# Graph layer with linear attention, 1 core: query denominators four chunks at a time in eight partitions, and the remainders of two weight slabs on VectorE

## The reference, cut to what matters

```python
phiQ = elu_plus_one(Q)                      # Q = xn @ Wq.T + bq, heads of 64
phiK = elu_plus_one(K)
S = jnp.einsum('bhki,bhkj->bhij', phiK, V)
Z = phiK.sum(axis=-2)
num = jnp.einsum('bhqi,bhij->bhqj', phiQ, S)
denom = jnp.einsum('bhqi,bhi->bhq', phiQ, Z)[..., None] + EPS
context = (num / denom).transpose(0, 2, 1, 3).reshape(B, L, E)
```

## Time and profile before

| | |
|---|---|
| median of three timed runs | 995.62 us |
| the profiled execution | 995.84 us |
| its span | 994.1 us |
| TensorE matmul busy | 975.2 us, 98% |
| VectorE | 543.9 us, 55% |
| ScalarE | 293.6 us, 30% |
| GpSimd | 142.4 us, 14% |
| bytes moved by DMA | 86.78 MB |
| query chunks | about 296 to 425 us |

### The profile page before, as it was taken

How to read it: one execution, slowest core, us unless ns; L and a number is a source line. 1 busy time by engine, 2 the same in 40 slices (tenths; PEclk the granted TensorE clock), 3 DMA queues, 4 the chain that set the end, 5 groups by cost and what they waited for, 6 DMA issues and landing times.

```text
span 994.1 us, 13325 instructions
## 1 busy us (share of the span) xinstructions
PE 975.2 (98%) x4860; PEld 824.4 (83%) x4860; DVE 543.9 (55%) x1067; ACT 293.6 (30%) x585; POOL 142.4 (14%) x191
## 2 busy tenths in 40 slices
PE   5999999999999999999999999999999999999998
PEld 4887888888889989978786788767788999999986
DVE  6886578777763888782113556447557212122354
ACT  6873122232133343341213221114113312135300
POOL 7101001001011050050300000000201103064100
PEclk9999999999999999999999999999999999999999
DMA  7412013113021022122201465535422302010053
GB/s 269 150 49 86 5 30 117 28 31 100 16 77 36 26 90 73 52 69 95 96 12 55 147 204 172 157 119 186 170 80 90 123 1 85 1 43 1 22 190 139
DMA packets 46979, 86.78 MB, mean 87 GB/s; under 512 B 19036, under 2 KB 23388, under 8 KB 46896
## 3 DMA queue, kind: packets, MB, share of 16 engines
q1 hardware_dynamic: 38416, 57.28, 17.5%
q0 software_dynamic: 8480, 28.45, 8.7%
HBM read 61.62 MB, written 24.09 MB: 86 GB/s over the span
## 4 chain that ended last, share of the span: by engine, by line
PE 92%; DVE 3%; DMA 2%; ACT 1%; issue 1%; POOL 1%; SPq 0%; DVEq 0%; ACTq 0%; POOLq 0%
PE PS L1431 11%; PE PS L1433 11%; PE PS L1432 11%; PE PS L1552 9%; PE PS L1553 9%; PE PS L1554 9%; PE PS L1610 5%; PE PS L1612 4%; PE PS L1630 3%; PE PS L1631 3%; PE PS L1629 3%; PE PS L1471 2%; PE PS L1446 2%; PE PS L1683 2%; PE PS L1682 2%; PE PS L1681 2%
## 5 line engine op out<-in xcount | busy, mean ns | idle before, releaser
L1431 PE MATMUL PS<-ring,act_t 128*128 128x512 f32 (+1 forms) x480 | 194.7, 406 | 1.3 <-POOL ring L443 0.6
L1433 PE MATMUL PS<-ring,act_t 128*128 128x512 f32 (+1 forms) x480 | 190.7, 397 | 0.0
L1432 PE MATMUL PS<-ring,act_t 128*128 128x512 f32 (+1 forms) x480 | 190.3, 396 | 0.0
L1552 PE MATMUL PS<-act_t,ring 128*128 128x416 f32 (+1 forms) x432 | 159.3, 369 | 1.4 <-POOL ring L443 1.3
L1553 PE MATMUL PS<-act_t,ring 128*128 128x416 f32 (+1 forms) x432 | 152.2, 352 | 0.0
L1554 PE MATMUL PS<-act_t,ring 128*128 128x416 f32 (+1 forms) x432 | 151.7, 351 | 0.0
L1431 PEld LDWEIGHTS PS<-ring,act_t 128*128 128x128 f32 (+1 forms) x480 | 89.8, 187 | 23.9 <-POOL ring L443 1.6
L1433 PEld LDWEIGHTS PS<-ring,act_t 128*128 128x128 f32 (+1 forms) x480 | 89.5, 186 | 22.4
L1432 PEld LDWEIGHTS PS<-ring,act_t 128*128 128x128 f32 (+1 forms) x480 | 89.9, 187 | 21.2 <-issue 0.5
L1552 PEld LDWEIGHTS PS<-act_t,ring 128*128 128x128 f32 x432 | 81.3, 188 | 6.8 <-issue 3.4
L1553 PEld LDWEIGHTS PS<-act_t,ring 128*128 128x128 f32 x432 | 81.4, 188 | 4.0 <-issue 3.4
(11 more groups left out here) (195 smaller groups left out, 1650.7 us busy)
## 6 DMA issues: line engine op xcount, KB each, us to landing
stage_x<-in_wslices_dram POOLq DMA_DIRECT2D x54, 256.0 KB, 4.2
stage<-in_wslices_dram POOLq DMA_DIRECT2D x42, 256.0 KB, 3.7
xr<-x_d SPq DMA_DIRECT2D x18, 512.0 KB, 3.6
phin_d<-phiq SPq DMA_DIRECT2D x8, 625.0 KB, 3.1
xrow<-in_x_dram SPq DMA_DIRECT2D x9, 512.0 KB, 3.6
xh<-in_x_dram SPq DMA_DIRECT2D x18, 256.0 KB
x_d<-xh SPq DMA_DIRECT2D x18, 256.0 KB
x_d<-xr SPq DMA_DIRECT2D x9, 512.0 KB, 3.0
```

Of the source, the lines that this page charges most:

```text
L1431: pe.matmul(out_ap, node_rows(0, k, t), ring[:, slot(k0 + k), 0, :], start=(k == 0), stop=False)
L1432: pe.matmul(out_ap, node_rows(1, k, t), ring[:, slot(k0 + k), 0, :], start=False, stop=False)
L1433: ins = pe.matmul(out_ap, node_rows(0, k, t), ring[:, slot(k0 + k), 1, :], start=False, stop=(k == KD - 1))
L1552: pe.matmul(out_ap, w[0], x_t[:, 0, k, o:o + n], start=(k == 0), stop=False)
```

## The change

- The key sums take one column per feature tile and are split into high half and remainder (`z_hl`, eight columns for each chunk's place in its group; the unused ones are zero). `phi_split` (ScalarE) and `phi_rest` (VectorE) split phiq into `phi_hl` (two buffers).
- A chunk's denominator is three fp32r passes with eight stationary columns. Four chunks of the same rows of x (four feature tiles) form a group and add into eight partitions of one bank. The order of the chunks changes to `q_chunk`; chunks 11 and 23 are still the last of their slab.
- Copy and reciprocal run once for a group, on eight partitions. The reciprocals go to DRAM (`rec_d`) and come back spread over 64 partitions a head, in four parts with a semaphore each. The multiply of chunk i is 8 chunks behind; phiq has nine buffers of a chunk, each stored by itself.
- Remainders of slices 42 to 57 are made by VectorE, eight after q_add(10) and eight after q_add(22). GpSimd keeps the loads. ScalarE makes all eight high halves ahead of its step of chunk 11 (23).

```diff
-PHI_BUFS = 3
+PHI_BUFS = 9
+PHI_LAG = 8
+def q_chunk(i):
+    s, r = divmod(i, 12)
+    return 4 * s + r % 4, r // 4
...
@@ sync
+            def rec_store(g):
+                n = CHUNKS[g % 3][1]
+                sp.wait_ge(rec_ready, g + 1)
+                sp.dma_start(rec_d[g].rearrange("a b n -> (a b) n")[:, 0:n], rec[0:8, 0:n]).then_inc(rec_stored, 16)
+            def rec_spread(g, j):
+                n = CHUNKS[g % 3][1]
+                sp.wait_ge(rec_stored, 16 * (g + 1))
+                if g >= 1:
+                    sp.wait_ge(phin_ready, 4 * (g - 1) + j + 1)
+                for h in range(2):
+                    sp.dma_start(rec_all[64 * h:64 * h + 64, j, 0:n],
+                                 rec_d[g, j, h:h + 1, 0:n].to_broadcast([64, n])).then_inc(rec_in[j], 16)
+            for i in range(24 + PHI_LAG):
+                g, late = divmod(i - 6, 4)
+                if late == 0 and 0 <= g < 6:
+                    rec_store(g)
+                if i >= PHI_LAG:
+                    phin_store(i - PHI_LAG)
+                if late == 0 and 0 <= g < 6:
+                    for j in range(3):
+                        rec_spread(g, j)
+                if late == 1 and 0 <= g < 6:
+                    rec_spread(g, 3)
...
@@ gpsimd
-            slab_rest(42)
-            slab_rest(50)
+            for n in range(42, 58):
+                reload(n)
...
@@ scalar
+            def phi_split(i):
+                n = CHUNKS[q_chunk(i)[1]][1]
+                act.wait_ge(phiq_ready, i + 1)
                 if i >= 2:
+                    act.wait_ge(phi_used, i - 1)
+                nc.scalar.activation(phi_hl[:, 0, i % 2, 0:n], phiq[:, i % PHI_BUFS, 0:n], ACT.Copy).then_inc(phi_hi, 1)
...
                 if i % 12 == 11:
-                    for k in range(42 + 8 * (i // 12), 48 + 8 * (i // 12)):
+                    for k in range(42 + 8 * (i // 12), 50 + 8 * (i // 12)):
                         hi(k)
...
-                if i >= 2:
-                    den_copy(i - 2)
+                if i >= 1:
+                    phi_split(i - 1)
+                if i >= 5 and i % 4 == 1:
+                    den_copy((i - 5) // 4)
...
+            phi_split(23)
             act.wait_ge(deg_copied, 1)
...
@@ vector
+            def phi_rest(i):
+                n = CHUNKS[q_chunk(i)[1]][1]
+                dve.wait_ge(phi_hi, i + 1)
+                dve.tensor_tensor(phi_hl[:, 1, i % 2, 0:n], phiq[:, i % PHI_BUFS, 0:n],
+                                  phi_hl[:, 0, i % 2, 0:n].bitcast(F32), ALU.subtract).then_inc(phi_lo, 1)
...
             for i in range(24):
                 q_min(i)
-                if i >= 3:
-                    den_invert(i - 3)
+                if i == 1:
+                    z_rest()
+                if i >= 1:
+                    phi_rest(i - 1)
+                if i >= 6 and i % 4 == 2:
+                    den_invert((i - 6) // 4)
+                if i >= PHI_LAG:
+                    den_apply(i - PHI_LAG)
                 q_add(i)
-                if i >= 3:
-                    den_apply(i - 3)
+                if i % 12 == 10:
+                    for n in range(42 + 8 * (i // 12), 50 + 8 * (i // 12)):
+                        weight_lo(dve, n)
...
             for t in range(NT):
                 h_lo(0, t)
-                if t < 3:
-                    den_invert(21 + t)
-                    den_apply(21 + t)
+                if t == 2:
+                    den_invert(5)
+                if t < PHI_LAG:
+                    den_apply(24 - PHI_LAG + t)
...
@@ tensor
-                for i in range(2):
-                    u = UNIT["z", i]
-                    b = open_unit(u)
-                    for j in range(4):
-                        ins = pe.matmul(PS[:, b, P * j:P * (j + 1)], ksum[:, P * (4 * i + j):P * (4 * i + j + 1)], ones[:],
-                                        start=True, stop=True)
-                    ins.then_inc(acc_full, 1)
+                u = UNIT["z", 0]
+                b = open_unit(u)
+                for f in range(KD):
+                    ins = pe.matmul(PS[:, b, f:f + 1], ksum[:, P * f:P * (f + 1)], ones[:, 0:1], start=True, stop=True)
+                ins.then_inc(acc_full, 1)
...
             def denominator(i):
...
+                pe.wait_ge(phi_lo, i + 1)
+                if j == 0 and g >= 2:
+                    pe.wait_ge(den_read, g - 1)
+                for z, b in ((0, 0), (0, 1), (1, 0)):
+                    ins = pe.matmul(PS[0:8, 3 + g % 2, 0:n], z_hl[:, z, i // 12, 8 * j:8 * j + 8], phi_hl[:, b, i % 2, 0:n],
+                                    start=(j == 0 and z + b == 0), stop=(j == 3 and z == 1))
+                ins.then_inc(phi_used, 1)
```

More of the change, by code:

```diff
@@ L108, in rows @@
     return min(P, N - t * P)
+def q_chunk(i):
+    s, r = divmod(i, 12)
+    return 4 * s + r % 4, r // 4
 def units():
     u = [("kv", s, t) for s in range(4) for t in range(NT)]
-    u += [("q", 0, 0), ("z", 0), ("z", 1)]
-    u += [("q", f, c) for f in range(KD) for c in range(3) if f or c]
+    u += [("q", 0, 0), ("z", 0)]
+    u += [("q", *q_chunk(i)) for i in range(1, 24)]
     u += [("h", 0, t) for t in range(NT)]
@@ L219, in build @@
         with ExitStack() as r2:
+            sb("pad3", [P, 2 * NT * 512 - 4 * 418], F32, r2)
+            phi_hl = sb("phi_hl", [P, 2, 2, 418], F32R, r2)
+        with ExitStack() as r2:
             hs = sb("hs", [P, 2, NT, 512], F32R, r2)
@@ L321, in build @@
         phiq_ready = sem("phiq_ready")
-        den_done = sem("den_done")
+        z_hi = sem("z_hi")
+        phi_hi = sem("phi_hi")
+        phi_lo = sem("phi_lo")
+        phi_used = sem("phi_used")
+        rec_stored = sem("rec_stored")
+        rec_in = [sem(f"rec_in{j}") for j in range(4)]
         den_read = sem("den_read")
@@ L498, in _ @@
                         keys_load(dt + KEY_BUFS)
-                if step >= 40 and (step - 40) % 3 == 2 and (step - 40) // 3 >= 1:
-                    phin_store((step - 40) // 3 - 1)
-            phin_store(KD - 1)
+            for i in range(24 + PHI_LAG):
[9 more added lines that the diff above has]
+                    rec_spread(g, 3)
             for b in range(PHI_BUFS):
-                sp.wait_ge(phin_stored[b], 16 * len(range(b, KD, PHI_BUFS)))
+                sp.wait_ge(phin_stored[b], 16 * len(range(b, 24, PHI_BUFS)))
             for b in range(2):
@@ L684, in _ @@
             for b in range(PHI_BUFS):
-                pool.wait_ge(phin_stored[b], 16 * len(range(b, KD, PHI_BUFS)))
+                pool.wait_ge(phin_stored[b], 16 * len(range(b, 24, PHI_BUFS)))
             for b in range(2):
@@ L1207, in q_add, with z_rest @@
                                   ALU.add).then_inc(phiq_ready, 1)
[L1209 to L1212, removed]
-            def den_apply(i):
[L1215 to L1219, removed]
+            def z_rest():
+                u = UNIT["z", 0]
+                dve.wait_ge(z_hi, 1)
+                for g in range(2):
+                    o = slice(64 * g, 64 * g + 64)
+                    z_out = dve.tensor_tensor(z_hl[o, 1, :, g:g + 31:10], PS[o, bank(u), 0:KD].rearrange("p (a b) -> p a b", a=2),
+                                              z_hl[o, 0, :, g:g + 31:10].bitcast(F32), ALU.subtract)
+                z_out.then_inc(acc_free[bank(u)], 1)
@@ L1220, in den_apply @@
+            def den_apply(i):
+                n = CHUNKS[q_chunk(i)[1]][1]
+                dve.wait_ge(rec_in[i % 4], 32 * (i // 4 + 1))
+                dve.tensor_tensor(phiq[:, i % PHI_BUFS, 0:n], phiq[:, i % PHI_BUFS, 0:n], rec_all[:, i % 4, 0:n],
                                   ALU.mult).then_inc(phin_ready, 1)
@@ L1234, in _ @@
                     dve.tensor_copy(deg[0:last, 0, NT - 1:NT], PS[0:last, 7, NT - 1:NT]).then_inc(deg_copied, 1)
+            phi_rest(23)
             dve.wait_ge(root_deg, 1)
```

85 lines of the change are left out of this document (42 added, 43 removed).

## The result

The changed kernel takes 1012.81 us (median of six runs, 1011.86 to 1013.65) where the kernel before took 996.51 (six runs, 995.32 to 998.20). The ratio is 1.0163, with a 95% interval of 1.0152 to 1.0173: slower, by 16 us where I had forecast 2.5. The profiled execution of the changed kernel has a span of 1010.9 us, that of the kernel before 994.1: +16.9 us.

A forecast was written before the change was run, and what follows sets the result against it. TensorE, busy for 98% of the span, was taken as the bound. Slab changes +6.2, passes −3.4 and key sums −0.3 gave +2.5 us: 998.3 us for the profiled execution, 998.1 as median, range 995.5 to 1003.

The forecast's parts named there:

- part 3: Remainders of both slab changes on VectorE: +9.77 us of TensorE waits, −3.54 us of GpSimd waits gone, net +6.23 us.
- Rival (b): At the slab changes phi_rest(10) comes in time, only 2.3 us of weight waits remain: 990.8 us, faster; chance 0.07.
- (d): Rival: the waits are real but 1 to 3 us smaller altogether, 996.5 us, no difference to be told; chance 0.12.
- part 1: Denominators on TensorE as three fp32r passes: 0.14 us saved each, 3.4 us in all; key sums 0.3 us.
- Rival (c): The eight-column passes of the denominators save nothing: 1001.5 us; chance 0.06.
- the key sums: TensorE's sixteen passes with one moving column instead of 128: 0.3 us saved, bounds 0 and 1.1 us.
- part 2: Inverse per group and its spread through DRAM: hidden; at the end, the last store before GpSimd's loads, nothing or 0.3 us.
- rival (a): TensorE's clock drops to half behind the 3.6 us waits, 4 us each: one 1002, both 1006; chance 0.12.

The follow-up runs named there:

- x1_early_switch: Changed kernel plus one GpSimd tensor_tensor on one column right behind the partition_all_reduce; 1002.67 us, ratio 1.0060 to the kernel before.
- x3_dve_rest_only: Kernel before with the remainders of slices 42 to 57 moved to VectorE, fp32 denominators kept; 992.04 us, ratio 0.9954.
- x4_filler: x1_early_switch plus twelve unused 416-column passes ahead of the wait in denominator(10) and in denominator(22); 998.48 us, ratio 1.0023 to the kernel before.
- x6_order: x1_early_switch with VectorE reordered: inverse ahead of phi_rest, remainders split four, two and two; 989.65 us, ratio 0.9934 to the kernel before.
- x2_gpsimd_rest: Changed kernel with the remainders of slices 42 to 57 back on GpSimd; 1001.68 us, ratio 1.0061 to the kernel before.
- x8_gpsimd_rest_inv_first: x2_gpsimd_rest with VectorE's inverse ahead of phi_rest; 997.31 us, ratio 1.0010 to the kernel before.
- x5_lag3: x1_early_switch with each denominator one chunk later and the group copies one step later; 992.03 us, ratio 0.9958 to the kernel before.

## Why the prediction was wrong

**Right: the waits at the slab changes (part 3).** The chain was forecast as first remainder 6.27 us after q_min(10), 0.80 us apart, q_min(11) at 12.46, phi_rest(10) from 14.74. VectorE's timeline of the changed kernel:

```profile
353.42 0.65 DVE L1233 TENSOR_SCALAR qmin<-PS,bq_sb 128x416 f32<-128x416 f32 x1 [1.30 <-PE PS L1611]
355.63 0.59 DVE L1258 TENSOR_TENSOR phi_hl<-phiq,phi_hl 128x416 fp32r<-128x416 f32 x1 [1.55 <-ACT phi_hl L858]
356.14 2.73 DVE L1264 RECIPROCAL rec<-rec 8x416 f32<-8x416 f32 x1
...
359.75 1.47 DVE L460 TENSOR_TENSOR ring<-stage,ring 128x512 fp32r<-128x512 f32 x2
361.32 4.67 DVE L460 TENSOR_TENSOR ring<-stage_x,ring 128x512 fp32r<-128x512 f32 x6
365.90 0.65 DVE L1233 TENSOR_SCALAR qmin<-PS,bq_sb 128x416 f32<-128x416 f32 x1
368.10 0.59 DVE L1258 TENSOR_TENSOR phi_hl<-phiq,phi_hl 128x416 fp32r<-128x416 f32 x1 [1.55 <-ACT phi_hl L858]
```

Measured from 353.42: 6.33, 12.48 and 14.68. Chunk 12 lost 10.50 − 5.12 = 5.38 us (forecast 5.40), h(0,0) 10.86 − 6.14 = 4.7 (4.4). Net of the old stalls the two are +6.6 us (5.38 + 4.72 − 3.54), forecast +6.2. Rival (b) didn't come about, nor did (d). That the inverse keeps its length with eight partitions (2.73 us) was right too.

**Right: the passes (part 1).** 5.12 to 5.13 us a chunk, 0.14 less than before in each. Rival (c) is out: three passes with eight stationary columns still step at 0.19 us. The Trainium skill, page "TensorE: Matmul & The Clock Gate", section "LDWEIGHTS (loading the stationary operand)", has a weight load go by its columns. The records of the loads are shorter with eight columns than with 128 (88 ns for 188, median), though by far less than in proportion, and the step of the passes doesn't change with them. The formula that I had taken from the section "Back-to-back issue gap" of that page of the Trainium skill is given there for a single pass by itself, not for a stream of passes. The saving that I worked out from it, 4.3 us, is 4.4 if added up rightly, and the measured one is 3.3. **A small miss:** the key sums saved nothing, 303.08 − 301.37 = 1.71 us for 1.70; I had taken 0.3.

**Wrong: the end of part 2, "Nothing, or 0.3 us".** This is the step that cost most: the term was put at nothing, and h(1,0) took 9.9 us longer. I checked that the last store would land before GpSimd's remainders were due, and took GpSimd to be ready from then on. But taking slices 42 to 57 from it in part 3 also took away its first elementwise instruction behind the all-reduce, and with it the early moment at which the gap behind the configuration records passed unseen. That gap, 9.4 us, is about 9 of the 9.9 us: x1_early_switch brings h(1,0) from 15.58 back to 6.63. The remaining 1.0 us is the store itself, which I had sized too small: GpSimd's loads were issued 4.8 us behind the end of the last multiply (482.58 to 487.42), not 3.1. The lateness of part 2 has a share in the large term too, since x3_dve_rest_only, with early loads, doesn't pay for the gap. The kernel before had a hint: 6.2 us ahead of its one all-reduce in which GpSimd waited for nothing in the profile. I asked neither what they were nor whether there were more on the way back.

**Wrong: the weight of rival (a).** I gave the lower clock 0.12 because the only idle time followed by a low clock in the trace was 8.6 us and the waits were to be 3.6 us. It came after both, and x4_filler, which takes most of the idle time away, doesn't have it. Its price was overstated, too: 2.6 and 1.5 us, not 4 us each, since the higher level was back at 374.7 and 442.8, less than 6 us behind the waits. With these 4 us in the main case the forecast would have been 1002, near the 1002.67 of x1_early_switch.

So the sum had +2.5 and came out as +6.6 for the slab changes, −3.3 for the passes, nothing for the key sums, +4.2 for the clock and +9.9 for h(1,0), together +17.4, of the +16.9 measured. The −0.5 us between them are spread over small differences that I can't assign.

## What to carry to other kernels

When work moves from one engine to another, look not only at what is queued behind it at its new place but also at what its old place did on the side: here the first elementwise instruction behind a GpSimd library call carried the switch of code, and without it, and with the loads behind it 34 us later (487.4 for 453.8), the switch fell into the critical stretch. Put a work item on a queue behind what the bounding engine asks for next, not ahead of it: with the same instructions and one small one more, x6_order is 0.7% faster than the kernel before where the changed kernel is 1.6% slower. And a wait of several microseconds on a TensorE at full pace should be priced with the passes behind it at half clock.

## What the runs showed of the hardware

- What I take for GpSimd's switch of code has no instruction in the profile, only a gap: 6.0 to 6.3 us ahead of partition_all_reduce, 7.8 us (in idle time) and 9.4 us (at 488.5 us, in the changed kernel) ahead of the tensor_tensor that follows. Its pair of records comes when the program reaches the next elementwise instruction, behind whatever DMA issues and their waits stand before it (488.5 us), but ahead of that instruction's own wait (309.5 us, for a remainder that starts at 357.45).
- Two waits of 3.5 us brought TensorE from 2.4 to 1.2 GHz; the same waits with 2.43 us of passes in them and 1.2 us of idle time left it at 2.4 GHz. A wait of 2.05 us in x1_early_switch was followed by the lower level too (659.5 to 662.9 us). So were rows of waits of 0.30, 0.75 and 0.59 us (x2_gpsimd_rest) and 0.55, 0.74 and 0.75 us (x8_gpsimd_rest_inv_first). Five waits of 0.47 to 0.63 us in h(0,0) of x2_gpsimd_rest weren't, nor were the short gaps at VectorE's pace in x5_lag3 (granted clock 1.00 from 360 to 375 us). Which of these rows lower the clock and which don't isn't explained by these runs.
- Passes with eight stationary columns keep the step of 0.19 us of passes with 128 at 416 moving columns, and sixteen weight loads of 128 columns with one moving column take 1.71 us, where with 128 moving columns they take 1.70.
- A GpSimd tensor_tensor that started beside VectorE's inverse on eight partitions took 4.27 us for 1.3 (x2_gpsimd_rest, at both slab changes), and the inverse wasn't slowed; beside an inverse on 128 partitions it took 1.28 to 1.30 us (kernel before). The other way round, a VectorE sum that starts during GpSimd's tensor_tensor takes 1.66 us for 0.58 (1.67 in the kernel before).
